# The subtraction that makes the second parts of q and k moves ahead of the output's addition and of two row maxima

## The chip, the core and the metric

One Trainium2 chip, one of its cores. The five engines TensorE (PE), VectorE (DVE), ScalarE (ACT), GpSimd (POOL) and SyncE (SP, which here issues transfers) each run their own instruction stream in program order and wait for each other on semaphores. The metric is the device time of one execution in microseconds (us); a change is compared with the kernel before on the same chip.

## The reference, cut to what matters

Eight stages over 2048 tokens of width 256: attention, mixture of experts, a small attention, attention and experts again, a recurrent "thought" stage, a banded attention, a second "thought" stage. The change touches the three large attentions. Two of them ("narrow" here) are causal over 512 tokens with 32 query heads and 8 key heads of 64, the third ("wide") attends within a band, with 16 query heads and 4 key heads of 128:

```python
q = (h @ wq).reshape(B, S, NHEADS, HEAD_DIM)
k = (h @ wk).reshape(B, S, KVHEADS, HEAD_DIM)
q, k = _rope(q, k)
scores = jnp.einsum('bqhd,bkhd->bhqk', q, k) / np.float32(np.sqrt(HEAD_DIM))
attn = jax.nn.softmax(jnp.where(causal[None, None], scores, -1e30), -1)
o = jnp.einsum('bhqk,bkhd->bqhd', attn, v).reshape(B, S, NHEADS * HEAD_DIM)
x = x + o @ wo
```

To keep accuracy, each factor of the products is split: a first part rounded to the matmul's format (`fp32r`) and a second part, the exact value minus the first. A product is then three matmuls (first by first, second by first, first by second).

## The kernel before

A `Plan` writes one list of steps; every engine's program walks that list in order and emits its own share of each step. So the place of a step in the list is the place of its instructions in every engine's stream.

**Units.** A narrow attention runs 16 units: 4 chunks of the heads times 4 batch rows. A unit has 8 steps: 4 tiles of 128 query rows times 2 key heads, 4 query heads each. The wide attention has 16 units of 4 steps. While a unit is attended, q, k and v of the next unit are prepared beside it, in "pieces": the generator `prepare` yields, and `beside()` takes its next piece at four places in each step (two pieces at each in the wide attention).

**Pieces.** Four pieces make the products and the rotation of a token tile (`products_of`: q and k/v on PE, rotation on DVE, sum on POOL into `p_tm`). Four pieces turn a tile (`turned_of`): PE transposes q into a PSUM bank (L1506), ACT copies out the first part (`p_q`, L1776), DVE subtracts to get the second part (L1946); the same for k (L1512, L1780, L1951). In a narrow unit, steps 0, 1, 3 and 5 hold products, steps 2, 4, 6 and 7 hold the turning of one tile each. In a wide unit, half of step 1 and of step 2 and all of step 3 hold turning.

**A narrow step.** In list order: scores of heads 0 and 1 with their row maxima on DVE (L1961); weighing with v of earlier probabilities (L1543); reciprocals; exponentials on ACT (L1786); then, in odd steps, DVE divides (L1984) and ACT and POOL split the result into parts (L1799, L2330); piece 1; then, in even steps, `project_out` (12 matmuls, L1559 to L1561; DVE adds to the residual `g_res`, L1992) and `spread` (PE transposes reciprocals, DVE copies them to `p_inverse_rows`, L1980; SP writes them to DRAM, L2450, and reads them back broadcast into `p_oT`, L2454, which the division of the next odd step multiplies by); piece 2; scores and maxima of heads 2 and 3; transposes of two tiles of earlier probabilities (L1534); exponentials; piece 3; the other transposes; piece 4.

**Banks.** Of the 8 PSUM banks, scores use 4 in the narrow attention. All else takes the other 4 in turn, so each use waits until the reader of the fourth use before has released its bank. In steps 2, 4 and 6 the order of uses is q transposed, project_out, spread, k transposed, then the probability transposes: the first of these waits for L1946, which frees q's bank. In step 7 it is weigh, q, k, then four probability transposes: the third waits for L1946 and the fourth for L1951. In a step with products, the bank of the k/v product is freed by the rotation's last instruction (L1941), and `project_out` of the next step takes it.

Of the kernel before, what the change touches and what calls it, by code (L numbers as in the profile page):

```python
# [7 lines left out]
P = 128  # L8
# [12 lines left out]
QW = 512  # L21
# [19 lines left out]
F32, F32R, BF16 = mybir.dt.float32, mybir.dt.float32r, mybir.dt.bfloat16  # L41
I32, U32 = mybir.dt.int32, mybir.dt.uint32
ALU, ACT, AX = mybir.AluOpType, mybir.ActivationFunctionType, mybir.AxisListType
# [113 lines left out]
class Plan:  # L157
# [121 lines left out]
    def attention(self, ph, wide, roomy, ahead):  # L279
# [3 lines left out]
        A = Phase()  # L283
# [3 lines left out]
        n = "L1_attn_" if wide else "L0_ffn_"  # L287
# [32 lines left out]
        s = self.step("attention_constants", A)  # L320
# [42 lines left out]
        if wide:  # L363
            sring, tring, wring = (Banks(self.banks[i:j]) for i, j in ((0, 2), (2, 4), (4, 8)))
        else:
            sring, tring = Banks(self.banks[0:4]), Banks(self.banks[4:8])
            wring = tring
# [31 lines left out]
        def prepare(c, b, unit):  # L399
            if c == 0:  # L400
                for _ in normed.pop(b):
                    pass
            unit.k, unit.v = k_st.take(), v_sb.take()
            unit.q, unit.q_made, unit.k_made, unit.v_made = [], [], [], []
            rotated = {}
            for t in range(T + 1):
                if t < T:
                    yield from products_of(c, b, unit, t, rotated)
                if t:
                    yield from turned_of(unit, t - 1, rotated[t - 1])  # L410
# [24 lines left out]
        def turned_of(unit, t, rotated):  # L435
            s = self.step("q_turn", A)
            s.tm, s.ready = rotated
            s.use, s.q = wring.take(), q_st.take()
            s.hi_made = self.scalar_made.up()
            yield  # L440
            k = self.step("k_turn", A)
            k.t, k.tm, k.q, k.q_use, k.q_hi = t, s.tm, s.q, s.use, s.hi_made
            k.use, k.k, k.hi_made = wring.take(), unit.k, self.scalar_made.up()
            s.tm.users.append(k.use.full)
            yield
            lo = self.step("k_low", A)
            lo.t, lo.use, lo.k, lo.hi_made = t, k.use, unit.k, k.hi_made
            unit.q.append(s.q)
            unit.q_made.append(s.use.free)
            unit.k_made.append(k.use.free)  # L450
            yield
            yield

# [137 lines left out]
        for n_u, (c, b) in enumerate(units):  # L591
            unit = made
# [1287 lines left out]
def vector_program(dve, plan):  # L1880
    w = Gate(dve)
    made = plan.vector_made.sem
    res = plan.res
    for s in plan.order:
        A = s.of
# [3 lines left out]
        elif s.kind == "statistics":  # L1889
            n = s.norm  # L1890
# [14 lines left out]
        elif s.kind == "normed":  # L1905
            n = s.norm
# [11 lines left out]
        elif s.kind == "normed_wide":  # L1918
            n = s.norm
# [5 lines left out]
        elif s.kind in ("q_rotate", "k_rotate"):  # L1925
# [3 lines left out]
            x = use.ap[:, 0:width].rearrange("p (h d) -> p h d", d=hd)  # L1929
# [10 lines left out]
            dve.tensor_tensor(b[:, :, 0:hf], x[:, :, hf:hd], s_left, ALU.mult)  # L1940
            dve.tensor_tensor(b[:, :, hf:hd], x[:, :, 0:hf], s_right, ALU.mult).then_inc(use.free[0].sem)  # L1941

        elif s.kind == "k_turn":
            x = s.q_use.ap.rearrange("p (j n) -> p j n", j=QW // P)
            w.wait_ge(s.q_hi, s.q.after)
            dve.tensor_tensor(s.q.ap[:, 4:8, :], x, s.q.ap[:, 0:4, :].bitcast(F32), ALU.subtract).then_inc(s.q_use.free[0].sem)  # L1946

        elif s.kind == "k_low":
            tok = cols(s.t * P, P)
# [5 lines left out]
        elif s.kind == "scores":  # L1955
            o = s.o
            w.wait_ge(A.masked)
            for h in s.heads:
                x = h.use.ap[:, 0:o.w]
# [34 lines left out]
        elif s.kind == "small_normed":  # L1994
            n, t = s.norm, s.t
# [27 lines left out]
        elif s.kind == "store_maxima":  # L2023
            x, two = A.nmax[:, s.qt % 2], A.nm_two[:, s.qt % 2]
# [18 lines left out]
        elif s.kind == "thought_normed":  # L2043
            n = s.norm
# [9 lines left out]
        elif s.kind == "thought_ln":  # L2054
            n = s.norm
# [32 lines left out]
        elif s.kind == "thought_out":  # L2088
            n = s.norm
# [27 lines left out]
        elif s.kind == "route_mean":  # L2117
            n = len(s.tiles)
# [12 lines left out]
        elif s.kind == "route_pick":  # L2131
            n = s.n
# [17 lines left out]
        elif s.kind == "route_place":  # L2150
            n = s.n
# [61 lines left out]
        elif s.kind == "list_spread":  # L2213
            n = LATER + 1
# [363 lines left out]
def build(nc, io, out):  # L2578
    ctx = ExitStack()
    plan = Plan(nc, io, out, ctx)  # L2580
    plan.whole()
    with nc.Block() as block:
        block.sync(lambda sp: sync_program(sp, plan))
        block.gpsimd(lambda pool: pool_program(pool, plan))
        block.vector(lambda dve: vector_program(dve, plan))
        block.scalar(lambda act: scalar_program(act, plan))
        block.tensor(lambda pe: tensor_program(pe, plan))
    ctx.close()
# [35 lines left out]
```

## Time and profile before

| | |
|---|---|
| median of 3 runs | 3961.35 us (3953.55 to 3968.76) |
| the profiled execution | 3989.86 us, its span 3988.1 us |
| TensorE clock granted, mean | 0.912 |
| busy: PE, DVE, ACT, POOL | 3396.4 us (85%), 2304.2 us (58%), 1928.5 us (48%), 1152.9 us (29%) |

The narrow attentions run from about 20 to 900 us and from about 1895 to 2790 us of the span, the wide one from about 3295 to 3870 us. PE is the busiest engine; a time is read by asking what PE waits for, and then what that waits for. In the timeline a row's start is exact and the modelled end of a matmul group overlaps the start of the next.

### The profile page before, as it was taken

The page shows a single profiled execution, that of the slowest core. Times are in us where ns is not written, and L with a number is a line of the kernel's source. Part 1 is how long each engine was busy: PE and PEld are TensorE (multiplying, and loading weights), DVE is VectorE, ACT ScalarE, POOL GpSimd, SP SyncE. Part 2 cuts the span into 40 slices and gives each one's busy share as a digit, 9 for nine tenths or more (in the row PEclk, how much of TensorE's full clock was granted, in tenths as well). Part 3 has the DMA queues.
Part 4 walks back from the last instruction along what each step waited for, and adds up shares of the span by engine and source line. Part 5 has one row for each costly group of instructions (what it writes and reads, how often), then busy time and mean ns, then how long its engine had stood idle before and what let it go on. Part 6 is the DMA issues. An engine that isn't in the chain of part 4 may idle for free. (4 is left out here: it accounts for less than half of the span.)

```text
span 3988.1 us, 63764 instructions
## 1 busy us (share of the span) xinstructions
PE 3396.4 (85%) x21130; PEld 2243.0 (56%) x21130; DVE 2304.2 (58%) x7805; ACT 1928.5 (48%) x5261; POOL 1152.9 (29%) x1088
## 2 busy tenths in 40 slices
PE   6899999887698698997789999988599667999976
PEld 4666666665454333343566666665355346788864
DVE  5555656553343676874566565555334366777766
ACT  4566666554122165665466666655322113555541
POOL 3323223343344100111232222243345342222213
PEclk9899999987899588999899999999799878999996
DMA  2023332111754422110102333211275510000010
GB/s 74 23 70 128 117 105 95 34 57 58 196 90 81 101 54 53 35 34 15 30 25 67 130 115 128 73 46 61 86 175 91 127 32 1 14 14 4 1 32 22
DMA packets 226444, 268.79 MB, mean 67 GB/s; under 512 B 25478, under 2 KB 196424, under 8 KB 225352
## 3 DMA queue, kind: packets, MB, share of 16 engines
q1 hardware_dynamic: 195176, 224.58, 18.5%
q0 software_dynamic: 30944, 40.14, 6.0%
q8 instruction: 174, 2.85, 0.3%
q14 instruction: 150, 1.23, 0.1%
HBM read 129.59 MB, written 134.25 MB: 66 GB/s over the span
## 5 line engine op out<-in xcount | busy, mean ns | idle before, releaser
L1961 DVE CUSTOM_DVE_ANT_0 bank<-bank,p_mask 128x256 f32<-128x256 f32 (+3 forms) x1280 | 581.5, 487 | 265.8 <-PE bank L1525 216.1
L1786 ACT ACTIVATE p_prob<-bank,p_small 128x256 f32<-128x256 f32 (+3 forms) x1280 | 645.5, 516 | 162.5 <-DVE p_small L1961 147.7
L1791 ACT ACTIVATE p_prT<-bank 128x512 f32<-128x512 f32 x752 | 420.8, 600 | 322.5 <-PE bank L1534 285.8
L1525 PE MATMUL bank<-p_k,p_q 64*128 64x256 f32 (+3 forms) x3840 | 533.6, 352 | 10.3 <-ACT p_prob L1786 9.2
L1534 PE MATMUL bank<-g_ident,p_prob 128*128 128x128 f32 x3008 | 437.5, 288 | 98.2 <-DVE p_q L1946 38.7
L1534 PEld LDWEIGHTS bank<-g_ident,p_prob 128*128 128x128 f32 x3008 | 338.5, 145 | 190.3 <-DVE p_q L1946 72.5
L1543 PE MATMUL bank<-p_prT,p_v 128*64 128x512 f32 (+1 forms) x1504 | 427.6, 602 | 7.7 <-ACT p_prT L1791 3.7
L2319 POOL TENSOR_TENSOR p_tm<-p_rope_a,p_rope_b 128x512 f32<-128x512 f32 x192 | 246.2, 1282 | 569.3 <-DVE p_rope_b L1941 547.5
L1525 PEld LDWEIGHTS bank<-p_k,p_q 64*128 64x128 f32 (+1 forms) x3840 | 343.5, 191 | 111.5 <-issue 70.0
L2330 POOL TENSOR_TENSOR p_oT_lo<-p_oT,p_oT_hi 128x512 fp32r<-128x512 f32 x128 | 163.9, 1281 | 822.5 <-ACT p_oT_hi L1799 666.9
L2020 DVE TENSOR_REDUCE p_nmax<-bank 128x1 f32<-128x512 f32 x512 | 325.1, 684 | 100.9 <-PE bank L1588 95.4
L1818 ACT ACTIVATE p_prT<-bank 128x512 f32<-128x512 f32 x512 | 278.0, 596 | 158.4 <-PE bank L1600 158.1
L1721 PE MATMUL bank<-p_w,p_hT 128*128 (+1 forms) x632 | 330.8, 606 | 0.1
L1498 PE MATMUL bank<-p_w_hi,p_aT_hi 128*128 128x512 f32 (+1 forms) x768 | 291.0, 379 | 26.1 <-DVE p_aT_lo L1903 25.8
L1786 ACT ACTIVATION_READ_ACCUMULATOR p_prob<-bank,p_small 128x1 f32 x1280 | 269.3, 210 | 0.0
L1500 PE MATMUL bank<-p_w_lo,p_aT_hi 128*128 128x512 f32 (+1 forms) x768 | 268.3, 349 | 0.0
L1499 PE MATMUL bank<-p_w_hi,p_aT_lo 128*128 128x512 f32 (+1 forms) x768 | 268.3, 349 | 0.0
L1559 PE MATMUL bank<-p_o_hi,p_oT_hi 128*128 128x256 f32 x768 | 236.8, 308 | 33.0 <-POOL p_oT_lo L2330 24.9
L1938 DVE TENSOR_TENSOR p_rope_a<-bank,p_cos 128x512 f32<-128x512 f32 (+1 forms) x384 | 186.1, 485 | 97.3 <-PE bank L1500 95.7
L1543 PEld LDWEIGHTS bank<-p_prT,p_v 128*64 128x64 f32 (+1 forms) x1504 | 126.8, 144 | 178.7 <-issue 157.2
L1984 DVE TENSOR_TENSOR p_oT<-bank,p_oT 128x512 f32<-128x512 f32 x128 | 88.3, 690 | 240.5 <-DMA p_oT<-inverse_saved 126.7
L1560 PE MATMUL bank<-p_o_hi,p_oT_lo 128*128 128x256 f32 x768 | 226.3, 295 | 0.0
(296 smaller groups left out, 6441.4 us busy)
## 6 DMA issues: line engine op xcount, KB each, us to landing
sorted<-p_blank SPq DMA_DIRECT2D x32, 2304.0 KB, 13.0
p_oT<-inverse_saved SPq DMA_DIRECT2D x256, 128.0 KB
p_w<-in_L_ffn_w SPq DMA_DIRECT2D x96, 256.0 KB, 4.6
p_h_in<-sorted SPq DMA_DIRECT2D x158, 144.0 KB
p_k_st<-k_saved SPq DMA_DIRECT2D x16, 288.0 KB
p_q_st<-q_saved SPq DMA_DIRECT2D x16, 288.0 KB
g_stage<-in_L_ffn_wq SPq DMA_DIRECT2D x8, 512.0 KB, 4.9
g_stage<-in_L_ffn_wo SPq DMA_DIRECT2D x16, 256.0 KB, 6.1
```

The source lines that it names most:

```text
L1498: pe.matmul(use.ap[:, 0:n], hi, whi[:, k, cols(c0, n)], start=k == 0, stop=False)
L1499: pe.matmul(use.ap[:, 0:n], lo, whi[:, k, cols(c0, n)], start=False, stop=False)
L1500: ins = pe.matmul(use.ap[:, 0:n], hi, wlo[:, k, cols(c0, n)], start=False, stop=k == KC - 1)
L1525: ins = pe.matmul(h.use.ap[:, 0:n], q[rows, at, :], k[rows, kp, o.g, keys], start=i == 0, stop=i == 2)
L1534: ins = pe.transpose(s.use.ap[:, j * P:(j + 1) * P], o.probs[j].ap[:, s.kt * P:(s.kt + 1) * P], ident[:, :])
L1543: ins = pe.matmul(s.use.ap[cols(o.g * A.hd, A.hd), :], o.u.v.ap[:, o.k0 + kt, cols(o.g * A.hd, A.hd)], o.prT[kt].ap, start=kt == 0, stop=k ...
L1721: ins = pe.matmul(o.up.ap, o.hT.ap[:, k * P:(k + 1) * P], w_all(A)[:, bass.ds(at + k * 2 * H, 2 * H)], start=k == 0, stop=k == KC - 1)
L1786: act.activation(s.prob.ap[:, 0:s.o.w], s.use.ap[:, 0:s.o.w], ACT.Exp, bias=sm[:, 0, j:j + 1], scale=-1.0, accum_out=sm[:, 1, j:j + 1]).th ...
L1791: act.activation(s.prT.ap, s.use.ap, ACT.Copy).then_inc(s.use.free[0].sem)
L1818: act.activation(s.pt.ap, s.use.ap, ACT.Exp).then_inc(s.use.free[0].sem)
L1961: dve.tensor_tensor_reduce(x, x, A.mask[:, A.mask.shape[1] - o.w:], -1.0, FAR, ALU.add, ALU.min, o.sm.ap[:, 0, h.j:h.j + 1]).then_inc(made)
L2020: dve.tensor_reduce(A.nmax[:, s.qt % 2, s.t, s.r, s.g % 2:s.g % 2 + 1], s.use.ap, axis=AX.X, op=ALU.max, negate=True).then_inc(s.use.free[ ...
```

## The change

Before, DVE's share of piece 1 is empty. Piece 2 holds q's second part, piece 3 k's second part. The change gives q's second part a step of its own, `q_low`, in piece 1, and puts `k_low` into piece 2 beside `k_turn`. The instructions, their operands and their counts stay; only their places in DVE's stream move. PE, ACT, POOL and SP keep their order.

```diff
             s.use, s.q = wring.take(), q_st.take()
             s.hi_made = self.scalar_made.up()
+            lo = self.step("q_low", A)
+            lo.use, lo.q, lo.hi_made = s.use, s.q, s.hi_made
             yield
             k = self.step("k_turn", A)
-            k.t, k.tm, k.q, k.q_use, k.q_hi = t, s.tm, s.q, s.use, s.hi_made
-            k.use, k.k, k.hi_made = wring.take(), unit.k, self.scalar_made.up()
+            k.t, k.tm, k.use, k.k, k.hi_made = t, s.tm, wring.take(), unit.k, self.scalar_made.up()
             s.tm.users.append(k.use.full)
-            yield
             lo = self.step("k_low", A)
             lo.t, lo.use, lo.k, lo.hi_made = t, k.use, unit.k, k.hi_made
             unit.q.append(s.q)
             unit.q_made.append(s.use.free)
             unit.k_made.append(k.use.free)
+            yield
             yield
             yield
```

DVE's stream in a step 4 (steps 2 and 6 are alike), from the reciprocals to the maxima of heads 2 and 3; `p_q` is q's second part, `g_res` the output's addition, `p_inverse_rows` the copy that starts the transfers, `p_k` k's second part, `ISA bank,p_small` a row maximum. Before:

```order
L1976 RECIPROCAL p_inverse<-p_small 128x4
L1992 TENSOR_TENSOR g_res<-bank,g_res 128x256
L1980 COPY p_inverse_rows<-bank 8x128
L1946 TENSOR_TENSOR p_q<-bank,p_q 128x512
L1961 ISA bank,p_small<-bank,p_mask 128x384
L1961 ISA p_small 128x1
L1961 ISA bank,p_small<-bank,p_mask 128x384
L1961 ISA p_small 128x1
L1951 SCALAR_TENSOR_TENSOR p_k<-bank,p_k 128x2x128
```

And after (line numbers are one higher):

```order
L1977 RECIPROCAL p_inverse<-p_small 128x4
L1947 TENSOR_TENSOR p_q<-bank,p_q 128x512
L1993 TENSOR_TENSOR g_res<-bank,g_res 128x256
L1981 COPY p_inverse_rows<-bank 8x128
L1952 SCALAR_TENSOR_TENSOR p_k<-bank,p_k 128x2x128
L1962 ISA bank,p_small<-bank,p_mask 128x384
L1962 ISA p_small 128x1
L1962 ISA bank,p_small<-bank,p_mask 128x384
L1962 ISA p_small 128x1
```

q's second part now stands ahead of the addition and of the copy, and k's second part ahead of both maxima.

DVE's stream in a step 7, from the division (`p_oT`) to k's second part, before:

```order
L1984 TENSOR_TENSOR p_oT<-bank,p_oT 128x512
L1946 TENSOR_TENSOR p_q<-bank,p_q 128x512
L1961 ISA bank,p_small<-bank,p_mask 128x512
L1961 ISA p_small 128x1
L1961 ISA bank,p_small<-bank,p_mask 128x512
L1961 ISA p_small 128x1
L1951 SCALAR_TENSOR_TENSOR p_k<-bank,p_k 128x2x128
```

After:

```order
L1985 TENSOR_TENSOR p_oT<-bank,p_oT 128x512
L1947 TENSOR_TENSOR p_q<-bank,p_q 128x512
L1952 SCALAR_TENSOR_TENSOR p_k<-bank,p_k 128x2x128
L1962 ISA bank,p_small<-bank,p_mask 128x512
L1962 ISA p_small 128x1
L1962 ISA bank,p_small<-bank,p_mask 128x512
L1962 ISA p_small 128x1
```

Here only k's second part moves, ahead of both maxima: a step 7 has no addition and no copy.

## Rows read from the trace of the kernel before

**Rows 1.** Groups by line (busy us, mean ns | idle before, its releasers); waiters for L1951

```profile
L1534 PE MATMUL bank<-g_ident,p_prob 128*128 128x128 f32 x3008 | 437.5, 288 | 98.2 <-DVE p_q L1946 38.7 <-DVE p_k L1951 21.0 <-DVE p_rope_b L1941 20.4
...
  PE bank L1534: 21.0, 24
```

**Rows 2.** Timeline of a step 7: start us, us, engine, line, [idle before <-releaser]

```profile
485.02 1.75 PE L1534 MATMUL bank<-g_ident,p_prob 128*128 128x128 f32 x12
485.24 0.38 ACT L1780 ACTIVATE p_k<-bank 128x256 fp32r<-128x256 f32 x1
485.38 0.69 DVE L1946 TENSOR_TENSOR p_q<-bank,p_q 128x512 fp32r<-128x512 f32 x1 [1.18 <-ACT p_q L1776]
485.98 0.69 DVE L1961 CUSTOM_DVE_ANT_0 bank<-bank,p_mask 128x512 f32<-128x512 f32 x1
...
487.24 0.42 DVE L1951 SCALAR_TENSOR_TENSOR p_k<-bank,p_k 128x256 fp32r<-128x256 f32 x1
487.71 0.66 PE L1534 MATMUL bank<-g_ident,p_prob 128*128 128x128 f32 x4 [0.94 <-DVE p_k L1951]
```

**Rows 3.** Timeline of a step 2 and of what follows in steps 3 and 4

```profile
505.69 0.62 ACT L1776 ACTIVATE p_q<-bank 128x512 fp32r<-128x512 f32 x1
506.18 0.42 DVE L1992 TENSOR_TENSOR g_res<-bank,g_res 128x256 f32<-128x256 f32 x1 [1.06 <-PE bank L1561]
506.52 0.27 DVE L1980 COPY p_inverse_rows<-bank 8x128 f32<-8x128 f32 x1
506.72 0.67 DVE L1946 TENSOR_TENSOR p_q<-bank,p_q 128x512 fp32r<-128x512 f32 x1
...
507.44 0.66 PE L1534 MATMUL bank<-g_ident,p_prob 128*128 128x128 f32 x4 [0.49 <-DVE p_q L1946]
...
512.30 0.69 DVE L1984 TENSOR_TENSOR p_oT<-bank,p_oT 128x512 f32<-128x512 f32 x1 [2.45 <-DMA p_oT<-inverse_saved]
...
515.59 0.36 PE L1559 MATMUL bank<-p_o_hi,p_oT_hi 128*128 128x256 f32 x1 [0.55 <-DVE p_rope_b L1941]
```

**Rows 4.** Timeline of VectorE over three units: their step 7, and copies and divisions between

```profile
380.49 0.69 DVE L1946 TENSOR_TENSOR p_q<-bank,p_q 128x512 fp32r<-128x512 f32 x1 [1.18 <-ACT p_q L1776]
...
412.17 0.27 DVE L1980 COPY p_inverse_rows<-bank 8x128 f32<-8x128 f32 x1
...
418.43 0.69 DVE L1984 TENSOR_TENSOR p_oT<-bank,p_oT 128x512 f32<-128x512 f32 x1 [2.21 <-DMA p_oT<-inverse_saved]
...
432.95 0.69 DVE L1946 TENSOR_TENSOR p_q<-bank,p_q 128x512 fp32r<-128x512 f32 x1 [1.18 <-ACT p_q L1776]
...
454.09 0.27 DVE L1980 COPY p_inverse_rows<-bank 8x128 f32<-8x128 f32 x1
...
459.23 0.69 DVE L1984 TENSOR_TENSOR p_oT<-bank,p_oT 128x512 f32<-128x512 f32 x1 [1.80 <-DMA p_oT<-inverse_saved]
...
538.46 0.69 DVE L1946 TENSOR_TENSOR p_q<-bank,p_q 128x512 fp32r<-128x512 f32 x1 [1.18 <-ACT p_q L1776]
```

**Rows 5.** Timeline of steps 4, 6 and 7 of the same unit as Rows 3

```profile
517.13 0.59 ACT L1776 ACTIVATE p_q<-bank 128x512 fp32r<-128x512 f32 x1
...
517.69 0.27 DVE L1980 COPY p_inverse_rows<-bank 8x128 f32<-8x128 f32 x1
...
530.11 0.27 DVE L1980 COPY p_inverse_rows<-bank 8x128 f32<-8x128 f32 x1
530.57 0.69 DVE L1946 TENSOR_TENSOR p_q<-bank,p_q 128x512 fp32r<-128x512 f32 x1 [0.18 <-ACT p_q L1776]
...
536.58 0.69 DVE L1984 TENSOR_TENSOR p_oT<-bank,p_oT 128x512 f32<-128x512 f32 x1 [1.26 <-PE bank L1543]
```

**Rows 6.** Busy time by stretch, in the wide attention: PE, PEld, DVE, ACT, POOL, PEclk

```profile
3500.00:3600.00 100.00, 98.32 (x631) 81.13 (x629) 74.77 (x278) 55.49 (x171) 26.94 (x26) 1.00 0.05 14
```

**Rows 7.** Busy time by stretch (the same columns), in the second narrow attention

```profile
2220.00:2223.00 3.00, 1.66 (x13) 1.48 (x12) 2.39 (x14) 2.51 (x12) 2.56 (x2) 0.93 0.03 5
2223.00:2226.00 3.00, 3.00 (x16) 2.21 (x15) 1.98 (x8) 0.90 (x3) 0.73 (x1) 0.50 0.01 1
```

More of the change, by code:

```diff
@@ L1941, in vector_program @@
             dve.tensor_tensor(b[:, :, hf:hd], x[:, :, 0:hf], s_right, ALU.mult).then_inc(use.free[0].sem)
[L1943 to L1946, printed above, removed]
+        elif s.kind == "q_low":
+            x = s.use.ap.rearrange("p (j n) -> p j n", j=QW // P)
+            w.wait_ge(s.hi_made, s.q.after)
+            dve.tensor_tensor(s.q.ap[:, 4:8, :], x, s.q.ap[:, 0:4, :].bitcast(F32), ALU.subtract).then_inc(s.use.free[0].sem)
         elif s.kind == "k_low":
```

## The prediction

> **What bounds the kernel now.** I first read the groups of instructions by line and looked at what PE waits for. The transposes of the probabilities [rows 1] are preceded by 98.2 us of PE idle time; 38.7 us of it ended with q's second part (L1946) and 21.0 us, in 24 waits, with k's (L1951). These 60 us, 1.5% of the span, are what the change aims its two moved instructions at. Then I read the timeline to see why these two are late, and what stands behind them on DVE. The reader should see a step 7, where k's part alone matters, and a step 2, where q's part competes with the copy that starts a transfer.
>
> In a step 7 [rows 2] k's first part is ready at 485.24 + 0.38 = 485.62, but k's second part runs at 487.24, behind two maxima of 0.6 us each. PE waits for it until 487.71, idle 0.94 us.
>
> In a step 2 [rows 3] DVE is idle 1.06 us until project_out is done, then adds (506.18), copies the reciprocals (506.52) and only then takes q's second part (506.72), whose first part was ready at 505.69 + 0.62 = 506.31. PE waits 0.49 us for it. But the copy at 506.52 starts the write and the read of the reciprocals, and the division at 512.30 waits for that read: DVE is idle 2.45 us before it. The rotation stands behind the division, and at 515.59 project_out waits (0.55 us) for the rotation's last instruction. So two chains meet in PE here: the bank of q, and copy, transfers, division, rotation.
>
> **Is that second chain really the limit?** The trace holds a test. The time from one step 7 to the next is one unit [rows 4, 2]: 432.95 to 485.38 is 52.43 us, and 485.38 to 538.46 is 53.08, 0.65 longer. In the first the copy of step 2 (454.09) is followed by its division (459.23) after 5.14 us, in the second (506.52 to 512.30) after 5.78, 0.64 longer. The unit takes over the delay one to one. I read: after a step 2 the copy is on the path that sets the end, with a slack of at most 0.05 us. The copy of step 4 is not. The unit from 380.49 to 432.95 took 52.46 us, though its step 4 needed 418.43 − 412.17 = 6.26 us; so some 1.1 us of lateness is free there.
>
> **The change, part by part.** Nothing is added or removed, so only places count. On DVE an instruction takes its place for: q's second part 0.60 us (485.38 to 485.98), the addition 0.34 (506.18 to 506.52), the copy 0.20 (506.52 to 506.72) [rows 2, 3].
>
> *Step 7, k's second part.* It now follows q's at 485.98 and is done at 485.98 + 0.42 = 486.40, before PE has issued the third group of transposes (its x12 group ends at 486.77 as modelled). The wait of 0.94 us goes. The modelled end overlaps the next start by some 0.2 us, so a gain of 0.94 to 1.15; over the 24 waits 21.0 us to 26 us. I take 26. The two maxima move back by some 0.35 us; the exponentials that need them follow, but their banks and probabilities are used only in the next step, where PE first has a product and project_out to do. I take nothing for that.
>
> *Step 2, q's second part.* It starts at 506.31 + 0.04 = 506.35 (in steps where DVE waits for this copy, it starts that long after it) and the addition at 506.95 and not at 506.18. The copy goes from 506.52 to 507.29, 0.77 later. PE's wait of 0.49 shrinks to about 0.15, yet this gain is swallowed: PE arrives earlier at the same late bank. With 0.05 of slack a unit loses 0.72. There are 24 such steps in which the copy would be held up (28 in all, 4 of them have the first part so early, or the division so late, that nothing moves): +17 us. The bounds are 0, if the copy had slack after all, and 24 × 0.85 = 20.
>
> *Step 4.* q's first part is ready at 517.13 + 0.59 = 517.72, so the copy goes from 517.69 to 517.76 + 0.60 + 0.34 = 518.70 [rows 5], 1.01 later. With the 1.1 us that are free this costs nothing where the transfers take the short time (5.14), and up to 1 us where they take the long one (6.26). Of the 55 intervals from copy to division in steps with this copy that end a wait for the transfer, 18 are above 5.7 us. A third of 24 × 0.8 is +6 us; from 0 to 19. PE's gain at q's bank is 0.13 each, −3 us.
>
> *Step 6.* Here DVE already waits for q's first part [rows 5], so q's second part keeps its place (530.57) and the copy falls behind it: from 530.11 to 530.57 + 0.60 + 0.34 = 531.51, 1.40 later. The division of step 7 now starts at 536.58, bound by PE and not by the transfer. With the short transfer it would be at 531.51 + 5.14 = 536.65, with the long one at 537.77: 0.07 or 1.19 late, and ACT's copy of q, q's second part and PE's third transpose queue behind it. Over 20 units, a third of them long: +8 us; from 1 to 20.
>
> A rule bears on these transfers. The Trainium skill, "DMA: Bandwidth & Descriptors", section "Anatomy of one DMA", gives each transfer a fixed cost of about 2 us. Two in a row and the copy's 0.27 us would be 4.3 us, an estimate by that page; step 6 would then keep 0.8 us to spare and the sum would be 6 to 8 us lower. The trace has 5.14, and I go by the trace.
>
> *Wide attention.* PE is 98.32 us busy in 100 [rows 6]; there is hardly a wait to remove. k's second part is short there (one key head) and moves ahead of the low parts and one maximum by some 0.2 us. DVE is 75% busy. I take +2 us, from 0 to 4.
>
> **Sum.** −26 + 17 + 6 − 3 + 8 + 2 = +4 us on the profiled execution's 3989.9 us, 0.1%. That execution is 0.7% above the median of the runs, so I put the same difference on 3961.35: 3965 us. Two sides of a trade, each near 30 us, nearly cancel.
>
> **Rivals.**
> *The copy has slack* (faster). If PE, arriving earlier, were the limit after step 2, the costs of steps 2, 4 and 6 would fall away. −26 − 3 and another 24 × 0.34 of the wait at 507.44: −37 us, 3924 us. For it: the DVE idle time before the copy is large, and the division waits behind other things in some units. Against it: the one-to-one answer of the unit to the transfer [rows 4]. Chance 0.20.
>
> *The clock answers to the new waits* (slower). The late division makes PE wait twice within 3 us, about 0.4 to 0.7 us for the bank of the weighing and 0.6 for the rotation. In one stretch with such waits PE was busy 1.66 of 3.00 us, and the granted clock of the next stretch was 0.50, the lower of its two levels, 1.2 GHz, with PE busy throughout [rows 7]. Work done at that level takes twice as long, so 3 us of it cost 1.5 us. From half of the 24 units on, 12 × 1.5 = 18 us, this alone passes the bound below; together with the sum, 3983 us, and with all transfers long 3995. Against it: the waits here are shorter than in that stretch. The Trainium skill, "TensorE: Matmul & The Clock Gate", section "A second HAM failure mode: psum-queue depth-cycling", has a kernel whose frequent short waits between banks made the clock alternate; by that, this rival would come true. The narrow units of the trace, with four waits each and the clock full, speak against it. Chance 0.18.
>
> *The change does nothing* (same): each moved instruction runs in time that DVE idles in anyway, and PE meets another wait in the same step for the same length. Then 3961 us. For it: much of DVE's idle time is in these places. Against it: in step 7 nothing else holds the fourth transpose. Chance 0.12.
>
> **Numbers.** The forecast has 0.50, its own range 3945 to 3985. What a measurement of this kernel can tell from no change is about 0.5%, 20 us. Of the forecast, 0.06 falls on faster and 0.08 on slower; the rest of it and the third rival make 0.48 for same. Faster: 0.20 + 0.06 = 0.26 (rounded down to 0.25 for a weak form of the first rival that ends within the bound). Slower: 0.18 + 0.08 = 0.26, and 0.01 for late transfers, 0.27. The range is 3924 to 3995: it reaches both rivals' values and leaves the extreme tails of both out.
>
> **What would show it.** Right: the wait of PE for L1952 (k's) in step 7 gone; the copy L1981 some 0.8, 1.0 and 1.4 us later in steps 2, 4 and 6, counted from ACT's copy of q; PE waiting longer for the division or the rotation after step 2, where it now waits for q's part; the unit near 52.5 us as before. Wrong: a unit of 51.5 us or less (the copy had slack), or a lower granted clock between 200 and 750 us, or a division in step 7 that waits for the transfer by much more than a third of a microsecond on average.

## The result and the profile after

The changed kernel takes 3981.66 us (median of 6 runs, 3978.21 to 3996.01) against 3961.32 us for the kernel before (6 runs, 3953.55 to 3968.76). The ratio is 1.0059, with a 95% interval of 1.0040 to 1.0079: slower by 0.6%, some 23 us (the two medians alone are 20.3 us apart). The forecast was 3965 us, no change; 3981.66 lies within its range of 3924 to 3995, but it is just beyond the 20 us that the prediction itself took as the least that can be told from no change.

The profiled execution of the changed kernel took 3996.01 us, its span is 3994.2 us and its mean granted clock 0.905 (before 0.912). It is the slowest of its six runs and has the lowest clock of them (0.907 to 0.912 in the others), so its rows show the change somewhat larger than the median does. Line numbers of the changed kernel are one higher than before. First the groups by line that answer to [rows 1]: busy time, mean ns of one, and the idle time ahead of them with what ended it.

```profile
L1535 PE MATMUL bank<-g_ident,p_prob 128*128 128x128 f32 x3008 | 442.8, 291 | 82.4 <-DVE p_q L1947 27.6 <-DVE p_oT L1985 24.3 <-DVE p_rope_b L1942 19.7
L1985 DVE TENSOR_TENSOR p_oT<-bank,p_oT 128x512 f32<-128x512 f32 x128 | 88.4, 690 | 327.9 <-DMA p_oT<-inverse_saved 275.8 <-PE bank L1544 51.7
L1947 DVE TENSOR_TENSOR p_q<-bank,p_q 128x512 fp32r<-128x512 f32 x192 | 132.5, 690 | 188.8 <-ACT p_q L1777 188.6
L1952 DVE SCALAR_TENSOR_TENSOR p_k<-bank,p_k 128x256 fp32r<-128x256 f32 (+1 forms) x192 | 70.1, 365 | 6.0 <-ACT p_k L1781 5.9
```

The change did what it aims at. PE idles 82.4 us ahead of the transposes and not 98.2 us, k's part has left the list of what it waits for, and q's part stands at 27.6 us. But a new name is in the list: the division (L1985), 24.3 us. The division's own row tells why. It now ends 275.8 us of waiting for the transfer `p_oT<-inverse_saved`. In the kernel before, the same group reads:

```profile
L1984 DVE TENSOR_TENSOR p_oT<-bank,p_oT 128x512 f32<-128x512 f32 x128 | 88.3, 690 | 240.5 <-DMA p_oT<-inverse_saved 126.7 <-PE bank L1543 87.9 <-remote 18.7
```

The wait for the transfer has more than doubled. Next the timeline of the changed kernel, in a step 7 that answers to [rows 2] (start, length, engine and line; in brackets the idle time before and what ended it):

```profile
496.54 0.38 ACT L1781 ACTIVATE p_k<-bank 128x256 fp32r<-128x256 f32 x1
496.68 0.69 DVE L1947 TENSOR_TENSOR p_q<-bank,p_q 128x512 fp32r<-128x512 f32 x1 [1.18 <-ACT p_q L1777]
497.29 0.41 DVE L1952 SCALAR_TENSOR_TENSOR p_k<-bank,p_k 128x256 fp32r<-128x256 f32 x1
497.42 0.77 PE L1535 MATMUL bank<-g_ident,p_prob 128*128 128x128 f32 x5 [0.38 <-DVE p_q L1947]
```

k's second part follows q's directly, and PE has no wait for it (the view ends within this group of transposes, which runs on without a gap). PE now waits 0.38 us for q's part here. Then step 2 of the same unit, which answers to [rows 3]:

```profile
516.68 0.59 ACT L1777 ACTIVATE p_q<-bank 128x512 fp32r<-128x512 f32 x1
...
517.30 0.69 DVE L1947 TENSOR_TENSOR p_q<-bank,p_q 128x512 fp32r<-128x512 f32 x1 [1.16 <-ACT p_q L1777]
517.91 0.41 DVE L1993 TENSOR_TENSOR g_res<-bank,g_res 128x256 f32<-128x256 f32 x1
518.05 0.66 PE L1535 MATMUL bank<-g_ident,p_prob 128*128 128x128 f32 x4 [0.21 <-DVE p_q L1947]
518.24 0.27 DVE L1981 COPY p_inverse_rows<-bank 8x128 f32<-8x128 f32 x1
...
525.15 0.69 DVE L1985 TENSOR_TENSOR p_oT<-bank,p_oT 128x512 f32<-128x512 f32 x1 [4.64 <-DMA p_oT<-inverse_saved]
...
525.90 0.66 PE L1535 MATMUL bank<-g_ident,p_prob 128*128 128x128 f32 x4 [1.99 <-DVE p_oT L1985]
```

PE's wait for q's part is 0.21 us and not 0.49. The copy starts 518.24 − 516.68 = 1.56 us after ACT's copy of q, where it started 506.52 − 505.69 = 0.83 after it. It is 0.73 us later, and what stood at 0.49 us ahead of the transposes stands at 1.99 us ahead of the transposes behind the division (this step has a long transfer, 6.91 us from copy to division). And steps 4 and 6, which answer to [rows 5]:

```profile
530.61 0.69 DVE L1947 TENSOR_TENSOR p_q<-bank,p_q 128x512 fp32r<-128x512 f32 x1 [1.24 <-ACT p_q L1777]
531.21 0.41 DVE L1993 TENSOR_TENSOR g_res<-bank,g_res 128x256 f32<-128x256 f32 x1
531.54 0.27 DVE L1981 COPY p_inverse_rows<-bank 8x128 f32<-8x128 f32 x1
...
536.67 0.69 DVE L1985 TENSOR_TENSOR p_oT<-bank,p_oT 128x512 f32<-128x512 f32 x1 [1.49 <-DMA p_oT<-inverse_saved]
...
544.02 0.69 DVE L1947 TENSOR_TENSOR p_q<-bank,p_q 128x512 fp32r<-128x512 f32 x1 [1.32 <-ACT p_q L1777]
...
544.96 0.27 DVE L1981 COPY p_inverse_rows<-bank 8x128 f32<-8x128 f32 x1
...
550.20 0.69 DVE L1985 TENSOR_TENSOR p_oT<-bank,p_oT 128x512 f32<-128x512 f32 x1 [1.43 <-DMA p_oT<-inverse_saved]
```

In step 7 the division (550.20) waited for TensorE before; it now waits 1.43 us for the transfer, 5.24 us after its copy.

**What the forecast had not looked at: step 0.** Nothing of the change stands in step 0, and I did not price it. But from the fifth unit of each narrow attention on, SP also issues transfers of 2304 KB that blank the sorted rows, two in most units, at the unit's start behind step 6's reads. The DMA queue of SP, in the kernel before and then in the changed one, about this start (start, length of the issue, what it moves; the first is the blanking, the second the small write of the reciprocals, the third the reads that wait for that write):

```profile
479.78 3.40 SPq L2539 DMA_DIRECT2D sorted<-p_blank  x2
492.73 0.29 SPq L2450 DMA_DIRECT2D inverse_saved<-p_inverse_rows  x1
496.12 1.09 SPq L2454 DMA_DIRECT2D p_oT<-inverse_saved  x2
```

```profile
492.11 3.27 SPq L2540 DMA_DIRECT2D sorted<-p_blank  x2
502.86 0.29 SPq L2451 DMA_DIRECT2D inverse_saved<-p_inverse_rows  x1
509.01 1.09 SPq L2455 DMA_DIRECT2D p_oT<-inverse_saved  x2
```

Before, the write of step 0 comes 492.73 − 479.78 = 12.95 us behind the blanking, and 3.39 us go by until the reads. After, it comes 10.75 us behind, and 6.15 us go by. Both parts of the change shorten the gap: step 6's copy is later and takes the blanking with it, and the gain of step 7 brings step 0's copy nearer. The second of the two blanking transfers lands 2.19 us after the write was issued in the first case and 5.89 us after it in the second, so the write meets their tail, and a longer piece of it after the change.

To see where the time lies I measured the periods from one step 7 to the next, as in [rows 4], in 19 units of the two narrow attentions (nine of the first and ten of the second: the first units and those with the router are left out), and for each step the interval from copy to division in 28 units (median, and in how many the division waited for the transfer):

```
                        19 units    step 0        step 2        step 4        step 6
before                  1015.6 us   7.81 ( 6)     5.19 (27)     5.20 (24)     6.48 ( 0)
after                   1031.8 us   8.87 (16)     5.21 (28)     5.24 (28)     5.25 (17)
```

### The profile page after: what moved, and what is told of

It reads as the page before. It is cut to its first block and busy times, and to the rows that moved or that the text cites. A ratio compares the mean times of both kernels' runs of the same rounds, so it can differ in the third digit from the quotient of the medians.

```text
span 3994.2 us, 63762 instructions
## 1 busy us (share of the span) xinstructions
PE 3411.2 (85%) x21128; PEld 2258.8 (57%) x21130; DVE 2305.9 (58%) x7805; ACT 1922.5 (48%) x5261; POOL 1152.4 (29%) x1088
## 5 line engine op out<-in xcount | busy, mean ns | idle before, releaser
L1535 PE MATMUL bank<-g_ident,p_prob 128*128 128x128 f32 x3008 | 442.8, 291 | 82.4 <-DVE p_q L1947 27.6
L1544 PE MATMUL bank<-p_prT,p_v 128*64 128x512 f32 (+1 forms) x1504 | 418.8, 601 | 0.3 <-ACT p_prT L1792 0.3
L1499 PE MATMUL bank<-p_w_hi,p_aT_hi 128*128 128x512 f32 (+1 forms) x768 | 292.6, 381 | 27.6 <-DVE p_aT_lo L1904 27.3
L1985 DVE TENSOR_TENSOR p_oT<-bank,p_oT 128x512 f32<-128x512 f32 x128 | 88.4, 690 | 327.9 <-DMA p_oT<-inverse_saved 275.8
L1947 DVE TENSOR_TENSOR p_q<-bank,p_q 128x512 fp32r<-128x512 f32 x192 | 132.5, 690 | 188.8 <-ACT p_q L1777 188.6
L1800 ACT ACTIVATE p_oT_hi<-p_oT 128x512 fp32r<-128x512 f32 x128 | 80.8, 631 | 313.9 <-DVE p_oT L1985 313.9
## 6 DMA issues: line engine op xcount, KB each, us to landing
sorted<-p_blank SPq DMA_DIRECT2D x32, 2304.0 KB, 13.1
```

Source lines behind the costliest of these rows:

```text
L1499: pe.matmul(use.ap[:, 0:n], hi, whi[:, k, cols(c0, n)], start=k == 0, stop=False)
L1535: ins = pe.transpose(s.use.ap[:, j * P:(j + 1) * P], o.probs[j].ap[:, s.kt * P:(s.kt + 1) * P], ident[:, :])
L1544: ins = pe.matmul(s.use.ap[cols(o.g * A.hd, A.hd), :], o.u.v.ap[:, o.k0 + kt, cols(o.g * A.hd, A.hd)], o.prT[kt].ap, start=kt == 0, stop=k ...
```

## The experiments

All versions are timed against the kernel before on the same chip. A figure in us after a ratio is that share of 3961 us. The record holds q's part and k's part as steps that are put into pieces of `turned_of`; most experiments move one line there.

**k's part alone early.** q's second part stays where it was, behind the copy.

```diff
 (against the changed kernel, in turned_of)
-            lo = self.step("q_low", A)          # ahead of the yield
-            lo.use, lo.q, lo.hi_made = s.use, s.q, s.hi_made
             k.t, k.tm, k.use, k.k, k.hi_made = ...
             s.tm.users.append(k.use.full)
+            lo = self.step("q_low", A)          # in the second piece
+            lo.use, lo.q, lo.hi_made = s.use, s.q, s.hi_made
```

> Undoes one part: q's second part stands again in piece 2, behind the addition and the copy, and only k's second part is early (piece 2, ahead of the two maxima). Theory (the late copy of steps 2, 4 and 6 costs what k's early place gains): the unit between two steps 7 falls from about 52.4 to 51.3 us, PE's 24 waits for k's part (21.0 us) are gone, the copies stand where they stood before; ratio to before 0.993 to 0.995. Rival (the delayed maxima of heads 2 and 3 are what costs): the ratio is that of the change, 1.004 to 1.008, or at best 1.000.

Measured: 3984.95 us against 4006.87, ratio 0.9953 (0.9935 to 0.9971). This half alone makes the kernel faster by 19 us. The 19 units take 1000.2 us, 0.8 us less each; the median of the 15 in which no weights are loaded falls from 52.5 to 51.2 us.

**q's part alone early.** q's second part ahead of the addition, k's behind the second pair's maxima as before.

```diff
             lo.t, lo.use, lo.k, lo.hi_made = t, k.use, unit.k, k.hi_made   # k_low
 ...
+            yield                                # ahead of k_low
 ...
-            yield                                # behind it
```

> Undoes the other part: q's second part in piece 1, ahead of the addition and the copy, k's second part in piece 3 as before. Theory: all of the cost and none of k's gain; units some 1 us longer than in the change, ratio to before 1.010 to 1.015. Rival (the maxima): the maxima are not behind k's part here, so the ratio is below that of the change, 1.000 or less.

Measured: 4044.35 us, ratio 1.0101 (1.0076 to 1.0126). The parts add: −0.47% and +1.01% make +0.54%, and the whole change has +0.59%. The cost is on q's side.

**The chain cut, with and without the change.** SP's reads fetch the factors of the division from a constant table and wait neither for the copy nor for the write of the reciprocals; the outputs are so not divided by their sums. The same transfers run, and DVE's order is untouched.

```diff
-            w.wait_ge(s.use.free, s.place_read)
-            sp.dma_start(s.place, s.rows.ap).then_inc(s.saved[0].sem, 16)
-            w.wait_ge(s.saved, s.x.after)
+            w.wait_ge(s.x.after)
 ...
-                row = s.place[g * KV:(g + 1) * KV, :].rearrange("j q -> (j q)").unsqueeze(0)
+                row = io["rope0_cos"].rearrange("s d -> (s d)")[g * KV * P:(g + 1) * KV * P].unsqueeze(0)
 ...   (the write follows behind the reads)
```

> The kernel before with the chain cut: the factors in p_oT are read from a constant table (so the attention's output is not divided by its sums) without waiting for the copy and the write of the reciprocals. The write itself is still made. Theory: the division never waits for a transfer; the gain is small, since in the kernel before the chain is only just the limit in step 2 (0.0 to 0.7 us a unit) and where blanking transfers meet it: ratio 0.990 to 0.998.

> The changed kernel with the same cut. If the change costs through the copy and its transfers, cutting the chain turns it into a gain: after_no_chain is faster than before_no_chain by 0.8 to 1.2% (k's wait of 26 us and q's of 8 us and more), ratio to before 0.980 to 0.990. If it costs through the maxima, the addition or the clock, it stays slower than before_no_chain by some 0.5%.

Measured: 0.9900 (0.9872 to 0.9929) for the kernel before so cut, 0.9816 (0.9790 to 0.9841) for the changed one. The second over the first is 0.9915 (0.988 to 0.995 by the two intervals). With the chain cut the same change makes the kernel faster by 0.85%, or 34 us. The division's rows, of the changed kernel so cut and of the one before so cut:

```profile
L1985 DVE TENSOR_TENSOR p_oT<-bank,p_oT 128x512 f32<-128x512 f32 x128 | 88.2, 689 | 167.7 <-PE bank L1544 116.1 <-remote 25.0 <-DMA p_oT<-in_rope_cos 20.8
```

```profile
L1984 DVE TENSOR_TENSOR p_oT<-bank,p_oT 128x512 f32<-128x512 f32 x128 | 88.1, 688 | 149.3 <-PE bank L1543 119.5 <-remote 20.7 <-DMA p_oT<-in_rope_cos 6.1
```

The division waits for TensorE now, hardly for transfers. What the change costs goes through copy, write, reads and division. Whatever else it does on DVE (the maxima that move back) or to PE's short waits is still done here, and the balance is a gain: a rival that leaves this chain out does not explain the result. (A lower clock that follows from the late division does not leave it out; see the rivals.)

**q's part early in one step only,** k's part early throughout. The piece that runs in steps 2, 4 and 6 is that of tile 0, 1 and 2.

```diff
 (against k's part alone early; here tile 0)
             s.hi_made = self.scalar_made.up()
+            if not wide and t == 0:
+                lo = self.step("q_low", A)
+                lo.use, lo.q, lo.hi_made = s.use, s.q, s.hi_made
             yield
 ...
-            lo = self.step("q_low", A)
-            lo.use, lo.q, lo.hi_made = s.use, s.q, s.hi_made
+            if wide or t != 0:
+                lo = self.step("q_low", A)
+                lo.use, lo.q, lo.hi_made = s.use, s.q, s.hi_made
```

> The version with k's part alone early, and q's second part put early again only in the piece that runs in step 2 of the narrow units (tile 0); in steps 4 and 6 it stays behind the copy. My theory (the copy's delay goes through the transfers into the unit): the copy of step 2 comes 0.8 us later, the division, already bound by the transfer, with it, and the plain unit grows by 0.8 us on the 51.1 us of the version with k early, to 51.9; over 24 units about 19 us, so a ratio near 1.000. The rival, in which only the step that had slack and meets the blanking (step 6) costs: ratio as with k alone, 0.995.

> The same with q's part early only in the piece of step 4 (tile 1). On k early alone the copy to division of step 4 ends a wait for the transfer in 24 of 28 steps. My theory of the prediction has 1.1 us free there and a price of 6 us: ratio 0.997. If nothing is free once k is early: the copy 1.0 us later in 24 units, 24 us, ratio 1.001.

> The same with q's part early only in the piece of step 6 (tile 2). The division of step 7 changes from one bound by TensorE (copy to division 6.5 us) to one that waits for the transfer (5.1 to 5.3). By the prediction's term, 8 us: ratio 0.997. If the later copy also pushes the write of step 0 further into the blanking transfers, the units with blanking grow by more than the plain ones, by 1 us or more each (14 of them), and the ratio is 1.000 or above.

Measured, with the difference to k's part alone. Each difference is uncertain by about 0.23%, 9 us, by its two intervals. The unit sums come from one execution each, on several chips (the kernel before has a median of 3961 us on one and 4007 on another), so I read them for where time lies and take its amount from the ratios:

```
                   ratio    interval            to k alone          19 units   in 4 of them
k alone            0.9953   0.9935 to 0.9971                        1000.2     229.0
q early, step 2    1.0004   0.9989 to 1.0018    +0.51%  +20 us      1017.3     228.2
q early, step 4    0.9957   0.9939 to 0.9975    +0.04%   +2 us      1004.7     227.7
q early, step 6    0.9988   0.9973 to 1.0003    +0.35%  +14 us      1012.9     231.0
all three          1.0059   1.0040 to 1.0079    +1.06%  +42 us      1031.8     234.7
```

Step 2 costs what its copy is late: 20 us in 28 units is 0.7 us each, for a copy 0.73 us later. Step 4 costs next to nothing, as it had the slack. Step 6 costs 14 us. The division's row of that version shows the wait for the transfer at 215.6 us, against 156.1 us with k's part alone:

```profile
L1989 DVE TENSOR_TENSOR p_oT<-bank,p_oT 128x512 f32<-128x512 f32 x128 | 88.3, 690 | 271.9 <-DMA p_oT<-inverse_saved 215.6 <-PE bank L1548 37.1 <-remote 18.7
```

```profile
L1985 DVE TENSOR_TENSOR p_oT<-bank,p_oT 128x512 f32<-128x512 f32 x128 | 88.3, 690 | 249.7 <-DMA p_oT<-inverse_saved 156.1 <-PE bank L1544 73.6 <-remote 19.5
```

In that version the interval of step 0 grows with it, from 8.05 to 8.82 us (median), though nothing was moved in step 0: the later reads of step 6 push the blanking nearer to the write.

**The blanking later, all at once.** The unit's blanking issued behind the spread of step 0 and not at the unit's start, in the kernel before, the changed one and that with k's part alone early.

```diff
-            if not wide and NU <= n_u < 3 * B:            # ahead of the steps
-                for e in range(...):
-                    self.clear(A, e)
 ...
+                if not wide and NU <= n_u < 3 * B and (t, g) == (0, 0):   # behind spread(prev)
+                    for e in range(...):
+                        self.clear(A, e)
```

> The kernel before with the blanking transfers behind the spread of step 0. In the kernel before the division of step 0 waits for PE in nearly all units, so there is little to gain there: 0.997 to 1.003. With this, what the later blanking does alone is told from what it does for the changed kernel.

> The changed kernel, with one thing moved: the two or three transfers that blank the sorted rows, issued at the start of units 4 to 11 of each narrow attention, are issued behind the spread of step 0 instead. Theory (they and the write of the reciprocals of step 0 now meet, since the copies of step 6 come later and that of step 0 earlier): copy to division in step 0 of these units falls back from 8.4 to 10 us to the 7.8 us at which PE is the limit; the division waits for PE; ratio to before 1.001 to 1.003, against 1.006 of the change. Rival (nothing but steps 2, 4 and 6): the ratio stays 1.004 to 1.008. The blanking transfers may then meet the transfers of step 2 instead, which would show as a longer step 2.

> Both: only k's part early, blanking transfers behind the spread of step 0. Theory: at least as fast as k_early, ratio to before 0.990 to 0.995. If the blanking transfers then meet those of step 2, it is slower than k_early.

Measured: 1.0063 (1.0041 to 1.0086), 1.0080 (1.0057 to 1.0102) and 1.0010 (0.9993 to 1.0027). Step 0 is mended in all three (7.80 us, none waits for the transfer), but the blanking now meets the transfers of step 2, whose interval grows to 7.46 us in the kernel before and 6.65 in the changed one. I had moved the collision and not removed it, so this test says only half of what I wanted: the kernel before loses 0.63%, the changed one 0.21%, which is within its uncertainty, and the difference between them goes from 0.59% to 0.17% (0.9985 to 1.0049 by the two intervals). That it shrinks fits the collision, but the interval does not exclude that it stayed.

**The blanking split.** One transfer of 2304 KB behind the spread of step 0, the next behind that of step 2, the third, where there is one, behind that of step 4.

```diff
+            cleared = iter(range(...))                     # ahead of the steps
 ...
+                if g == 0:                                  # behind spread(prev)
+                    for e in cleared:
+                        self.clear(A, e)
+                        break
```

> The changed kernel with the blanking transfers of a unit no longer issued all at its start but one behind the transfers of step 0, one behind those of step 2 and the third behind those of step 4. Each takes about 6.5 us of the DMA engines and some 9 us lie between a read and the next write, so if the write of step 0 behind the blanking is what the prediction missed, units with blanking fall to the plain unit's 52.4 us and the whole kernel by 14 times 2 to 6 us: ratio between 0.985 and 0.995 against the kernel before. If the large transfers slow whatever is near them, 1.000 to 1.008.

> The same spread of the blanking on the version with k's part alone early. It should keep that version's plain units of 51.1 us and take the stretched ones down to it: ratio 0.98 to 0.99, the fastest of all versions that compute the whole thing. If the transfers merely collide elsewhere, 0.995 to 1.001.

Measured: 3958.15 us, 0.9992 (0.9978 to 1.0006), for the changed kernel and 3921.37 us, 0.9899 (0.9878 to 0.9920), for k's part alone early. Neither of the first expectation's two ranges holds 0.9992; the second's does hold 0.9899. A blanking now lands after 8.7 us (median). In the changed kernel all but one have landed when the next write is issued. With k's part alone early the second of each unit is still in flight at the write of step 4, for another 0.4 to 2.1 us, and costs that write 1 us at most. The queue of SP in the second kernel, over three steps of a unit with blanking:

```profile
380.72 0.27 SPq L2455 DMA_DIRECT2D inverse_saved<-p_inverse_rows  x1
381.98 1.08 SPq L2459 DMA_DIRECT2D p_oT<-inverse_saved  x2
383.12 0.58 SPq L2544 DMA_DIRECT2D sorted<-p_blank  x1
394.85 0.27 SPq L2455 DMA_DIRECT2D inverse_saved<-p_inverse_rows  x1
396.12 1.09 SPq L2459 DMA_DIRECT2D p_oT<-inverse_saved  x2
397.26 0.58 SPq L2544 DMA_DIRECT2D sorted<-p_blank  x1
405.53 0.27 SPq L2455 DMA_DIRECT2D inverse_saved<-p_inverse_rows  x1
```

The first two writes are followed by their reads after 1.27 us. Step 0's interval is 7.80 us in all 28 units. By these two, the collision with the blanking was 0.67% of the changed kernel (1.0059 to 0.9992) and 0.54% of the one with k's part early (0.9953 to 0.9899). But q's part costs nearly as much without it: 0.9992 − 0.9899 = 0.93%, 37 us, against 1.06%. Of the 47 us between the two spans (3962.9 and 3915.8) about 14 lie in the stretch between the two narrow attentions, which took 1055.4 us in the second profile and 1069.1 in the first, and 1068.8 to 1074.3 in the others of the tables above; I have no cause for it. The 19 units have 999.2 and 979.5 us, 19.7 apart, where with the blanking in its old place they were 31.5 apart. So in these units some 12 of 31.5 us of what q's part costs was the collision. This is an estimate: the 19.7 come from one chip, the 31.5 from two.

This last version, k's part early and the blanking split, is faster than both kernels: by 1.0% than the one before.

## Why the prediction was right and wrong

**Step 7, −26 us.** The mechanism holds: PE's wait for k's part (L1951, 21.0 us) is gone, and a plain unit is shorter by 1.2 us, at or above the 0.94 to 1.15 that I gave it. The size was too large: 19 us measured (12 to 26 by the interval). The profile of k's part alone early shows where it was lost. The four of the 19 units in which weights are loaded beside the blanking took 225.2 us before and 229.0 there, while the other 15 gained 19.1 us, 1.3 each. In these four the intervals of step 0 grew from 11.73–12.92 us to 13.11–13.74: the write met the blanking sooner. So the sum gave all 24 units the gain, and some of them lost it again in step 0.

**Step 2, +17 us.** Right. The copy was 0.73 later (I had 0.77) and PE's wait 0.21 (0.15); the cost measured is 20 us. The one-to-one answer of the unit to the transfer in [rows 4] was the sound reading, and the experiment with this step alone confirms it.

**Step 4, +6 − 3 us.** Right: +2 us. The slack of 1.1 us was there.

**Step 6, +8 us.** Too small: 14 us, within my bounds of 1 to 20. The copy starts 544.96 − 543.39 = 1.57 us after ACT's copy of q and not 530.11 − 529.94 = 0.17, 1.40 later, as worked out. In the step of the timeline above the division then waited for the transfer, as it did in 17 of 28 units; I had a third. The transfer itself took about what I had put on it. With q's part early in step 6 alone, the intervals of step 6 in the 18 units from the third to the eleventh of each attention are together 5.9 us longer than the 5.07 at which TensorE sets the division. Those of step 0, where nothing was moved, grew by 12.5 us together against the version with k's part alone. What I left out is that step 6's reads are also what SP issues just ahead of the blanking. The section of the Trainium skill that the prediction cites here, "Anatomy of one DMA" in "DMA: Bandwidth & Descriptors", gives its 2 us for transfers that GpSimd issues; these are issued by SP, and the interval measured is 5.25 us (median) after the change.

**Step 0, not in the sum.** This is the step that failed. The working went through the steps whose order the change edits and stopped there; the gain of step 7 and the lateness of step 6 both arrive in step 0, and there they meet the blanking, with the reads of the reciprocals held for 6.15 us and not 3.39. The kernel lets step 0 wait for its transfer in 16 of 28 units, before in 6. In the 16 steps 0 that follow a blanking, the intervals exceed the 7.80 us at which TensorE sets the division by 17.3 us in all before, by 27.8 with k's part alone early, by 40.3 with q's part early in step 6 as well, and by 45.8 in the changed kernel: 28.5 more than before, where the result missed the forecast by 19. It explains both errors, the short gain and the long cost, in sign. In size the 19 units put about 12 us on it for q's part, and the four units with loads some 9 us for k's: 1.3 gained in each of the others against 0.95 lost, times four. The ratios give less, 1.06% against 0.93% for q's part, 5 us, with an uncertainty of over 10. That this collision took part is shown by the rows and by the split; how much of the 23 us is its share is not settled.

**The wide attention, +2 us.** Not tried by itself. From the last step 7 of the narrow units to the end of the span the kernel before took 1216.4 us and the changed one 1213.5. Nothing points to a cost. The measured parts, −19, +20, +2 and +14, make +17 us of the 23; the other 6 are within the uncertainty of the sum.

**The rivals.** *The copy has slack* has fallen for step 2: by the version of that step alone it would have been 0.995, and it was 1.0004. It holds for step 4. *The clock answers to the new waits* has come true in part; the forecast had put it at nothing in its sum, and a lower clock in this stretch was one of its own signs of being wrong. Here the rows for the stretch that I had named, of the kernel before and of the changed one (length; busy time and instructions of PE, PEld, DVE, ACT and POOL; the granted clock):

```profile
200.00:750.00 550.00, 514.54 (x3505) 358.35 (x3507) 324.63 (x1203) 354.21 (x1034) 146.81 (x127) 1.00 0.29 95
```

```profile
200.00:750.00 550.00, 512.23 (x3457) 356.81 (x3457) 321.04 (x1192) 347.04 (x1021) 146.64 (x127) 0.98 0.29 94
```

The clock is 0.98 and not 1.00. Over the 19 units, with the same matmuls in each version (length, busy time of PE, granted clock):

```
                                 19 units    PE busy    clock
before                           1015.6 us    948.3     0.993
k alone early                    1000.2       947.0     0.986
after                            1031.8       959.6     0.980
k alone early, blanking split     979.5       938.7     1.000
after, blanking split             999.2       947.5     0.997
```

The length times what is missing from 1.00 is the most that the clock can have cost, an estimate from these rows: 7 us before and 21 in the changed kernel, 13 of the 16 us by which its units are longer. The busy time of PE grew by 11. So the clock may carry a good part of the difference between these two profiles, and less of that between the medians, since the changed kernel's profile is its run with the lowest clock. It is no cause beside the chain. In the first three rows it falls as the waits of step 0 grow (17.3, 27.8 and 45.8 us above), with the blanking split it is nearly back, and in both versions with the chain cut it is 1.000. Nor does it carry what q's part costs: with the blanking split at most 3.4 of the 19.7 us between the two versions can be the clock's. And k's part alone early is faster than the kernel before at a lower clock.

*The change does nothing* has fallen by both halves.

Both sides of the trade had the right mechanism in the steps that the change edits, and both were off in the same direction: 7 us too much gain, and 8 us too little loss (36 against 17 + 6 − 3 + 8 = 28). Each error is about as large as the uncertainty of its measurement; their sum, with 23 us against 4, is not. The range held all the same, and the forecast's own range (3945 to 3985) with 3 us to spare. That was in part luck, as neither had room made in it for step 0. That the clock's rival had 3983 us, next to the 3981.66 measured, is chance too: its 18 us were to come from waits behind step 2, not from step 0. And the third of the prediction's signs of being wrong came as well: the division of step 7 waits 0.87 us for the transfer, as a mean of 28. Most of that is time in which it would have waited for TensorE; only some 0.2 us go beyond.

**What stays open.** How the 23 us divide between the later copies, step 0 and the clock is known only roughly. The four longest units, those with the router, seem to go the other way from the rest: 289.5 us before, 279.3 after, but 299.7 with k's part alone early and 297.0 with q's alone. These numbers go with the chip rather than with the change. On the chips where the kernel before has medians of 4004 to 4007 us, the eight versions with the chain whole take 294.6 to 302.9 us there; where it has 3961 to 3964 us, the three such versions take 271.9 to 279.3. What makes the chips differ is not known, and two of these three have the blanking split. The 14 us between the narrow attentions in one profile have no cause either, and the kernel before with the blanking split was not run, so what the change costs there is known only for q's part.

## What to carry to other kernels

When an edit makes one step of a repeating unit earlier or later, follow the shift once around the unit, through the steps that the edit does not touch, and through each transfer queue: a small transfer on which a chain waits can meet a large one that was issued at a time which another step sets. An instruction that starts a chain of dependent transfers (here 0.2 us of copy ahead of 5.2 us of write and reads) goes ahead of longer work on its engine, even where another engine waits for that work; move the two instructions of a change apart before you judge it, since one here was worth −0.5% and the other +1.0%. Large transfers with no hurry are best cut into pieces that end before the next small one is issued: the split alone turned the changed kernel from 1.0059 to 0.9992.

## What the runs showed of the hardware

The small write of the reciprocals, `inverse_saved<-p_inverse_rows`, and the issue of the reads behind it are 1.27 us apart where no blanking is in flight (380.72 to 381.98 above; the median of 112 in the kernel before, of which the longest took 2.6). Behind two transfers of 2304 KB on the same queue it took 3.39 us when issued 12.95 us after them and 6.15 when issued 10.75 after them; with the loads of weights ahead of the blanking as well it was 7.91 us in the kernel before:

```profile
322.81 4.82 SPq L2539 DMA_DIRECT2D sorted<-p_blank  x2
332.75 1.10 SPq L2450 DMA_DIRECT2D inverse_saved<-p_inverse_rows  x1
340.66 1.12 SPq L2454 DMA_DIRECT2D p_oT<-inverse_saved  x2
```

The Trainium skill, "DMA: Bandwidth & Descriptors", section "Queues, rings and completion order", has each DMA engine consume the descriptors of a queue in the order of its ring. These rows agree: in the 16 places of each of the two kernels where the write follows a blanking, the reads that wait for it start between 0.7 us before and 1.2 us after the second blanking transfer has landed, and in the pair of cases above they start 2.8 us later after a write that was issued 2.2 us sooner. That the order of the ring is the reason, and not that the engines are shared with other transfers, was not tried apart.

Of two transfers of 2304 KB issued together, the first lands after 8.7 to 12.0 us and the second after 14.1 to 17.8 us in the changed kernel; issued one at a time they land after 8.7 us (median). The page's rows of the changed kernel and of the same with the blanking split give the median of all of them, so the 13.1 us stand for neither of a pair:

```profile
sorted<-p_blank SPq DMA_DIRECT2D x32, 2304.0 KB, 13.1
```

```profile
sorted<-p_blank SPq DMA_DIRECT2D x32, 2304.0 KB, 8.7
```
